# Batch transposes of a two-tower feature kernel, from the fifth batch slice on in two halves on 64 rows of the array, with a unit between them

## The reference

```python
e = stack([tbl_f[ids[:, f]] for f in range(32)], axis=1)        # 1024 x 32 x 64
p, q = e[:, iu, :], e[:, ju, :]                                 # all pairs i < j
z = einsum('bpe,fpe,bpf->bp', p, kernel, q)                     # 1024 x 496
h = concatenate([z, dense_ctx], axis=1)                         # 1024 x 512
h = maximum(h @ W_top1 + b_top1, 0)                             # 512
h = maximum(h @ W_top2 + b_top2, 0)                             # 256
y = h @ W_top3                                                  # 1024 x 1
```

## Time and profile before

| | |
|---|---|
| Median of 3 runs | 483.64 us (479.96 to 483.74) |
| Profiled execution | 483.11 us, of which the span from first to last instruction is 481.3 us |
| PE busy | 411.4 us (85%) |
| DVE busy | 342.4 us (71%) |
| ACT busy | 325.4 us (68%) |
| POOL busy | 268.3 us (56%) |
| Mean granted TensorE clock | 0.957 of full |

### The profile page before, as it was taken

How to read it: one execution, slowest core, us unless ns; L and a number is a source line. 1 busy time by engine, 2 the same in 40 slices (tenths; PEclk the granted TensorE clock), 3 DMA queues, 4 the chain that set the end, 5 groups by cost and what they waited for, 6 DMA issues and landing times.

```text
span 481.3 us, 12047 instructions
## 1 busy us (share of the span) xinstructions
PE 411.4 (85%) x4144; PEld 280.4 (58%) x4144; DVE 342.4 (71%) x428; ACT 325.4 (68%) x2456; POOL 268.3 (56%) x308
## 2 busy tenths in 40 slices
PE   0554358888898988999999999999999999999997
PEld 0332245655556555767666666666666566666875
DVE  0044158889798878788778887888888788877820
ACT  1244215078967887689857897878786978988512
POOL 5757735566556555555545555556555555577400
PEclk9976568999998999999999999999999999999999
DMA  8751101015111111111111111111111111000000
GB/s 278 268 215 27 26 14 24 18 24 155 21 23 21 20 24 21 21 22 22 23 19 20 23 23 21 20 24 21 20 24 23 22 21 20 16 1 3 1 2 0
DMA packets 12756, 19.17 MB, mean 40 GB/s; under 512 B 6036, under 2 KB 6296, under 8 KB 12568
## 3 DMA queue, kind: packets, MB, share of 16 engines
q0 software_dynamic: 8192, 8.40, 9.4%
q1 hardware_dynamic: 2592, 8.29, 4.8%
q10 hardware_dynamic: 1912, 1.71, 1.2%
HBM read 18.39 MB, written 0.00 MB: 38 GB/s over the span
## 4 chain that ended last, share of the span: by engine, by line
PE 74%; DVE 12%; issue 9%; another core or an unknown queue 2%; DMA 2%; POOL 1%; ACT 1%; DVEq 0%
PE t_ps L570 25%; PE z_ps L642 14%; PE t_ps L600 12%; PE t_ps L587 9%; DVE prod L476 6%; PE prep_ps L657 5%; PE prep_ps L611 3%; DVE prod_a L498 2%; PE prep_ps L704 2%; DVE prod_a L517 2%; PE t_ps L657 2%; DVE zb L504 1%; DMA raw<-tbl,ids_sb 1%; POOL raw L356 1%
## 5 line engine op out<-in xcount | busy, mean ns | idle before, releaser
L356 POOL DMA_INDIRECT raw<-tbl,ids_sb x256 | 242.3, 946 | 172.5 <-issue 48.0
L418 ACT ACTIVATE prod_a<-prod_a 128x64 f32<-128x64 f32 x1184 | 283.9, 243 | 69.0 <-DVE prod_a L533 33.5
L418 ACT ACTIVATION_READ_ACCUMULATOR prod_a<-prod_a 128x1 f32 x1184 | 223.9, 189 | 7.5 <-issue 7.5
L476 DVE TENSOR_TENSOR prod<-t_ps,xt 128x1024 f32<-128x1024 f32 x128 | 155.7, 1220 | 63.6 <-PE t_ps L570 25.5
L570 PEld LDWEIGHTS t_ps<-xt,k_sb 64*128 64x128 f32 x2048 | 136.5, 193 | 55.3 <-issue 31.7
L570 PE MATMUL t_ps<-xt,k_sb 64*128 64x128 f32 x2048 | 151.7, 286 | 19.3 <-issue 10.1
L498 DVE TENSOR_TENSOR prod_a<-t_ps,raw 128x1024 f32<-128x1024 f32 x64 | 78.0, 1219 | 23.6 <-PE t_ps L600 14.7
L600 PE MATMUL t_ps<-k_sb,xt 64*128 64x512 f32 x256 | 74.7, 654 | 19.3 <-issue 14.1
L517 DVE TENSOR_TENSOR prod_a<-t_ps,raw 128x768 f32<-128x768 f32 (+2 forms) x96 | 62.9, 683 | 31.1 <-PE t_ps L587 24.0
L642 PE MATMUL z_ps<-prod,sel_sb 128*32 128x256 f32 x1024 | 71.7, 390 | 4.0 <-issue 3.7
L587 PE MATMUL t_ps<-k_sb,xt 64*128 64x384 f32 (+5 forms) x448 | 66.0, 402 | 3.5 <-issue 1.8
(11 more groups left out here) (30 smaller groups left out, 91.1 us busy)
## 6 DMA issues: line engine op xcount, KB each, us to landing
raw<-tbl,ids_sb POOLq DMA_INDIRECT x256
k_sb<-kmat SPq DMA_DIRECT2D x4, 768.0 KB
k_sb<-kmat SPq DMA_DIRECT2D x4, 512.0 KB
k_sb<-kmat SPq DMA_DIRECT2D x4, 448.0 KB, 4.6
k_sb<-kmat SPq DMA_DIRECT2D x4, 256.0 KB
w_sb<-w ACTq DMA_DIRECT2D x1, 1024.0 KB
w_sb<-w ACTq DMA_DIRECT2D x1, 512.0 KB
ids_sb<-ids SPq DMA_DIRECT2D x1, 128.0 KB, 2.4
```

What stands on the lines that cost most here:

```text
L356: nc.gpsimd.indirect_dma_start(raw[:, n % RING, begin:begin + EMBED], None, tables[2 * k + f], bass.IndirectOffsetOnAxis(ap=ids_sb[:, t, 2 ...
L418: last = nc.scalar.activation(product, product, ACT.Copy, accum_out=zb[:, unit[1], at:at + 1])
L476: nc.vector.tensor_tensor(prod[:, own].rearrange("p n (m b) -> p (n m) b", b=P), t_ps[:, slot].rearrange("p n (m b) -> p (n m) b", b=P), x ...
```

## The change

Fills whose first pack lies in slice five or later (the last 16 of the 47 fills, number 31 to 46) are cut in two. `half` stands where the fill stood and transposes the samples 0 to 63 of the four packs (rows 0 to 63 of `raw`, four transposes of 64 rows, 128 columns out, 64 samples each). The rest, samples 64 to 127 on rows 64 to 127, keeps the name `fill` and stands one unit later. The second part waits for the first on a new semaphore, `half_done`; the first waits on `prep_copied` as the fill did; both wait on `gathered`. ACT's copy, which goes with `fill`, moves one unit later too. In the period the order becomes `half, C, sums, fill, F, B, F, ...`: sums have rank 0.8 and the fill rank 1, so the second half comes after the sums. The first two of the 16 are the exception, `half, F, fill, B` and the like.

```diff
+def halved(j):
+    return FILLS[j][1][0] >= HALVED_FROM * PACKS
+HALVED_FROM = 4
...
     for j, (n, packs) in enumerate(FILLS):
-        at.append((n, 1, ("fill", j)))
+        if halved(j):
+            at += [(n, 1, ("half", j)), (n + 1, 1, ("fill", j))]
+        else:
+            at.append((n, 1, ("fill", j)))
...
+            def transpose_half(j, half):
+                if half == 0:
+                    pe.wait_ge(prep_copied, PREP_COUNT["fill", j] - 1)
+                else:
+                    pe.wait_ge(half_done, HALF_COUNT[j])
+                rows = slice(half * EMBED, (half + 1) * EMBED)
+                for n, p in enumerate(FILLS[j][1]):
+                    group, at = divmod(p, GROUP)
+                    pe.wait_ge(gathered[group % RING * GROUP + at], 32 * (group // RING + 1))
+                    begin = n * P + half * EMBED
+                    last = nc.tensor.transpose(prep_ps[:, begin:begin + EMBED],
+                                               raw[rows, group % RING, at * P:(at + 1) * P], ident_sb[rows, rows])
+                last.then_inc(prep_done if half else half_done, 1)
+
             def transpose_fill(j):
+                if halved(j):
+                    transpose_half(j, 1)
+                    return
```

More of the change, by code:

```diff
@@ L215 @@
 SCHEDULE = schedule()
+HALF_COUNT = {j: n + 1 for n, j in enumerate(x[1] for x in SCHEDULE if x[0] == "half")}
 PREP_COUNT = {use: n + 1 for n, use in enumerate(x for x in SCHEDULE if x[0] in ("fill", "turn", "piece"))}
@@ L239, in scalar_schedule @@
                 banks += [("sum", *x, n) for n in range(2) if n not in vector_sums(x)]
-        else:
+        elif x[0] != "half":
             if x[0] == "turn":
@@ L307, in build @@
         gathered = [sem(f"gathered{s}") for s in range(RING * GROUP)]
-        prep_done, prep_copied = sem("prep_done"), sem("prep_copied")
+        prep_done, prep_copied, half_done = sem("prep_done"), sem("prep_copied"), sem("half_done")
         t_done, prod_done, summed, z_copied = sem("t_done"), sem("prod_done"), sem("summed"), sem("z_copied")
@@ L727, in _ @@
                     turn_sums(x[1])
+                elif x[0] == "half":
+                    transpose_half(x[1], 0)
                 else:
```

## The result

The changed kernel takes 483.82 us (median of 20 runs, 482.02 to 489.17) where the kernel before takes 481.42 (20 runs, 479.84 to 483.74): a ratio of 1.0056, interval 1.0036 to 1.0075, so 2.7 us slower (the two medians differ by 2.4). 484.4 was predicted. That is within the 1% of "same", but the interval does not hold 1: the change costs a little. The profiled execution took 483.97 us.

The account below looks back on a forecast made before the run. Nearly PE-bound, with C often held by DVE: eleven held periods +2.2, five open -1.75, stream +0.3, together +0.75 us on the profiled 483.11, 483.9; with 0.53 to the median, 484.4. Range 479.0 to 490.0.

Parts of the forecast that it names:

- Held C units: C behind the fill waits for DVE's multiply in 11 of 16 periods; there the first half saves nothing.
- Rival A: PE is the bound everywhere and the multiply comes earlier: all 16 periods save 0.35 us, -5.3 us, 478.3; chance 0.12.
- The lag that I couldn't explain: DVE started the F unit of 301.13 1.2 us after PE's records of it ended at 299.96.
- A half's cost: Four 64-row transposes on PE at 0.06 us each: 0.24 us a half, from 0.20 to 0.44.
- The second half behind the sums: Between sums and F nothing hides it: F 0.20 us later a period (0.16 to 0.44), +2.2 us in eleven held periods.
- The open fills: In five periods C isn't held by DVE: 0.79 us of fill becomes 0.24, saving 0.55; net -1.75 us.
- The wait on `half_done`: PE ahead of the second half: set more than 1 us earlier, so over when PE comes to it.
- The copy: ACT's copy moves one bank sum later, ending at about 308.0, 0.9 us before the piece that waits; costed at nothing.
- Rival C: ACT's copy comes too late for the piece: some 0.4 us in 15 periods, 6 us, 490.4; chance 0.09.
- Rival B: PE's loads set the pace at 0.11 us each, a half costs 0.44 us: +5.8 us, 489.4; chance 0.13.
- A mode of its own: Half transposes drain like fills; second halves pay 0.10 to 0.20 us more each, 486.0 to 487.6; in the forecast's share.
- Instruction stream: 64 more loads and matmuls and 16 waits on PE, about 0.6 of a packet: +0.3 us (0 to 0.5).

Follow-up runs that it names:

- adjacent halves: Changed kernel, both halves where the fill stood, second directly behind first: 502.64 us, ratio 1.0464 to the kernel before; third chip, without gathers, 421.24 us, ratio 1.0010.
- whole fills and PE's own wait: Kernel before, plus a PE wait for its own `prep_done` behind each of the last 16 fills: 502.37 us, ratio 1.0296 to the kernel before.

## Why the prediction was right, and where it was mis-sized

- **The number itself: partly luck.** 484.4 against 483.82 looks like a hit to 0.6 us. But the sum had +0.75 us for the change and 2.7 was measured, and it stood on a median of three runs, 483.64, where 20 runs give 481.42. A change costed 1.9 us too low and a start 2.2 us too high cancelled.
- **Held C units: right, on wrong evidence.** The count of 11 held and five open fills is what the timelines show. The ten of the earlier trace rows don't show it: they are six C units behind fills, some seen twice, and two C units behind pieces, and that 8 + 2 came to the right count is luck. With the halves PE stands idle behind ten of the 16, and where it does, C starts 0.05 or 0.06 us behind the multiply. A doubled first half is hidden for the most part. Rival A falls on the first chips. On the third C was open in the kernel before, and there A's sign is the one that is seen, though 1.4 us and not 5.3.
- **The lag that I couldn't explain** is that of PE's increments. In the earlier trace rows the F unit of 298.90 ended at 299.96, its increment came at 301.04 and DVE started at 301.13; the C unit of 302.41 ended at 303.54, its increment came at 305.57 and DVE started at 305.67.
- **A half's cost: right.** Transposes are 0.06 us apart. With prompt increments the second half costs 0.24 us a period, and doubled it costs 0.24 more. The swap of F's load for the half's (0.04) that I took off does not show.
- **The second half behind the sums: the mis-sized term.** "So F is 0.24 - 0.04 = 0.20 us later" measured 0.31 to 0.42 us over 12 periods, by where one cuts, between my 0.20 and my upper end of 0.44, but not for the reason of that end (streams of 0.11 us). 0.24 is the half. The remaining 0.07 to 0.18 was seen only on the chips with late increments; the whole fill in that place pays 0.47 or more. That the place is to blame is shown (whole fill moved: 1.0061). Why a place just behind the sums pays more than its instructions there is not shown; PE's idle time named issue ahead of units of F's kind, between 215 and 432 us, was 4.0 us in 5 places in the kernel before and is 6.5 us in 16 in the changed one, which fits.
- **The open fills: right.** The first half's side gave 0.18 to 0.29 us a period, by where one cuts, against 0.17 costed. The three open fills of the 12 periods gave 0.45 to 0.47 us each between the start of the fill and the next unit. In one held period (fill of 314.50) C came free as well: 0.91 us from fill to C before, 0.12 changed, so the multiply came earlier there, a part of Rival A that I had at nothing.
- **The wait on `half_done`: wrong in part.** "The wait is over when PE comes to it" held behind the sums in later periods and failed in the first two fills, by 0.6 and 0.7 us. I had taken an increment to arrive with the end of its records; it came 1.4 to 3.5 us later in 15 of the 16. It cost some 0.5 us by the ratios (1.0056 against 1.0046, with intervals that overlap), but it decides every variant in which the second half stands nearer the first.
- **The copy: right here.** On ACT's timeline it ran from 306.87 to 307.47 us, and the piece started at 308.73. This period lies 0.55 us earlier than in the earlier trace rows (C at 301.86 for 302.41), so that is the 308.0 that I had worked out; the cover is 1.3 us, not 0.9. Rival C is real one bank sum further on: +23 us on the third chip.
- **Loads at 0.11 us (Rival B): did not happen.** The Trainium skill, "TensorE: Matmul & The Clock Gate", section "LDWEIGHTS (loading the stationary operand)", says that the number of rows doesn't matter; the trace agrees (139 ns from 64 rows, 140 from 128). Its figure, an estimated 107 ns for 128 columns, is not what paces these: four transposes lie within 0.40 us with the 0.22 of the last, so they follow each other after 0.06 us.
- **A mode of its own: no.** The first half starts 0.10 us behind the start of F's last record, and the records of half and unit overlap.
- **Instruction stream: one packet more**, as costed; it can't be told from the rest.

The sum redone on 16 periods: 16 x 0.13 = +2.1 us, and with the two waits at the start of it some 0.5 more, +2.6. The trace itself has +2.3 from the first changed fill to the last, and the runs measured 2.7.

## What to carry to other kernels

Before a step is cut in two, look for what holds the unit behind each part: a part hidden behind another engine's work gives nothing back when it gets cheaper, and a part moved to a spot where PE is late costs its whole length and here somewhat more, so try the move alone first. Bound also the wait that orders the two parts, by how long this kernel's increments take to arrive, and keep several microseconds of other work between them. The change cost 0.6% on one chip and, with the gathers left out, gained 0.4% on another, so compare runs on the same chip and say on which. And count waits on a timeline: a view that lists loads and matmuls apart shows one wait twice.

## What the runs showed of the hardware

- Semaphore increments of PE arrived late on the first chips while gathers were made: `half_done` of the changed kernel 1.4 to 3.5 us after the end of the records that raise it, the whole fill's `prep_done` in the kernel before 1.1 to 3.2 us (15 of 16 each; the last of each, made after the gathers, 0.01 us), those of the units 1.0 us in the median before and 0.9 changed. On the third chip they arrived after 0.01 to 0.04 us in the median. The same kernel took 481 to 482 us on the first chips and 420.79 us on the third, with PE busy 85% of the span before and 93% in the trace without gathers. What makes them late is open: on the first chips it ends with the gathers, on the third gathers made none late, and no kernel without gathers was run on the first.
- A PE that waits for its own increment pays for it 16 times over on the chip with late increments: 481.22 x 0.0464/16 = 1.4 us a period with adjacent halves and 481.22 x 0.0296/16 = 0.9 with whole fills and PE's own wait, by their ratios.
- The Trainium skill, "TensorEngine Tiling (Array Packing)", section "Gotcha 1: PSUM Pressure", says that different row tiles can't access the same PSUM bank at the same time and that software must ensure synchronization. `half_done` does that here, and no run left it out. With adjacent halves on the third chip it cost some 0.2 us: of the five transposes from 264.24 on the last starts at 264.24 + 0.73 - 0.27 = 264.70, where a pace of 0.06 us puts it at 264.48. In the period shown on the second chip it cost 2.2 us.
- Records of different row halves overlap: F's first record starts 0.01 us behind the first of the second half's transposes (305.61 and 305.62).
